# A mixture of experts in two stages: zero-filled half tile, early transposes, mask by expert, and first expert weights moved into the front stage

## Chip, cores and metric

One core of one Trainium2 chip runs the whole program. The metric is the device time of one execution in microseconds (us); less is better. The kernel of before took 2925.15 us, the median of three runs (2924.38 to 2936.98).

## What is computed

Input x has 16 sequences of 512 tokens with 256 features, 8192 tokens in all, in fp32. Four blocks follow each other:

```
x = x + attention(layernorm(x))        # 16 heads of 16
x = x + ffn(layernorm(x))
x = x + forget_attention(layernorm(x))
x = x + ffn(layernorm(x))              # the same weights again
```

The change concerns `ffn`, a mixture of E = 64 experts with F = 192 hidden features beside one shared expert with 192:

```
logits = x @ router_w.T;  the 8 largest of softmax(logits), normalised to sum 1
each expert takes the first 128 tokens (C = 128) that chose it, in order of tokens
y = (silu(xb @ w_gate) * (xb @ w_up)) @ w_down      # for each expert
out = sum over a token's experts of weight * y
    + (silu(x @ gate) * (x @ up)) @ ws_down         # shared expert
```

## The kernel before, in words

`program` calls seven stages one after the other; each has its own tiles, and all engines meet between two. `mixture` (L1755) is called twice and runs `moe_front` (tag m1f, later m2f) and `moe_experts` (m1e, m2e).

**`moe_front`** works in 16 rounds of 4 tiles of 128 tokens. Every engine walks the same steps s = 0 to 27 with the helper `in_turn`: for each step it goes through its own list of (step of item i, stage, number of items) and issues what is due. So the order of the list is the order of an engine's queue inside a step. Round i is loaded at step i, normalised and turned at i+1, has its logits at i+2 and its mask counted at i+3. The shared expert of round r runs gate and up at `shared_at(r)`, which is 2r+2 for the first eight rounds and r+10 for the others, and its down projection one step later. So in the first half (steps 2 to 18) even steps have gate and up and odd steps down; from step 19 on each step has one round of both, and two groups of four experts for the slot search.

The pieces: `turn_x` (L977) transposes x on TensorE in two halves of a round through the one bank `ps_x`; ScalarE's `keep` (L935) copies each half into `x_turned`, which holds all 8192 tokens. `logits` (L987) multiplies it by the router's weights. VectorE's `eight_largest`, `mark`, `shift` and `choose` (L866 to L883) make the 0/1 mask `chosen`, laid out as tile by expert. `count_tiles` (L996) sums the mask over tiles into `ps_c`, with `chosen` as the moving operand. `gate_up` (L1004) has 192 gate and 192 up features in three 128-wide groups; the third holds 64 of each. So `hidden` (L894) writes a product with 128 rows and one with 64, and `down` (L1016) contracts first over 128 rows (L1022), then over the 64 rows `hT[0:SR]` (L1023).

The slot search finds the token of each of 128 slots of each expert. `reach` (L902, VectorE) compares the counts with the slot numbers, 16 groups. `climb` (L1027, TensorE) multiplies an expert's mask, as weights, by two triangular tables, into `ps_x`; `copy_rise` (ScalarE) copies that; `find_place` (L1037) multiplies by `reached` into the one bank `ps_l`; `count_below` (L908, VectorE) reduces it. `count_reached` (L1046) multiplies `reached` by ones for all 64 experts, into `ps_c`, at step 20. The queue of SP carries the loads of x (`load`), the loads of the residual, the stores of the normalised rows with their gates, and the stores of the result. POOL sets constants first, then makes the inverse deviations, the gates and the last addition.

**`moe_experts`** handles 32 pairs of experts, pipelined by the lags of L1075: pair i's match of slots at step i+2, x turned at i+3, gate and up at i+4, h turned at i+5, down at i+6, scatter at i+7. SP loads a pair's weights (three DMAs of 384 KB, L1128 and L1129) into a ring of eight, as soon as down of eight pairs earlier is done. POOL gathers the 128 rows of each expert by an indirect DMA (L1139) and adds the outputs to the result in HBM by two indirect DMAs a pair (L1149). A scatter of pair i waits until all scatters before it have landed (L1146), and ScalarE's and VectorE's copies of y (a ring of four, YB) wait for the scatter of four pairs earlier. TensorE's order in a step is on L1202:

```
in_turn([(L_DOWN, down_second), (L_TURN, turn), (L_GU, gate_up(0)), (L_DOWN, down_first), (L_GU, gate_up(1)), (L_TURN_H, turn_h),
         (L_SAME, spread_first)])
```

`down_second` waits for ScalarE's copy of h (`copy_h`), which follows `turn_h` of the step before.

## Time and profile before

| What | us |
|---|---|
| median of 3 runs | 2925.15 |
| profiled execution | 2919.55 |
| its span | 2917.9 |
| TensorE matmuls busy | 2560.5 (88%) |
| VectorE busy | 1764.7 (60%) |
| ScalarE busy | 1255.0 (43%) |
| GpSimd busy | 1095.4 (38%) |

In the span, `moe_front` runs from 1247 to 1531 and from 2352 to 2629 us, `moe_experts` from 1534 to 1808 and from 2633 to the end. The other stages fill the rest. Engines in the rows: PE is TensorE's matmul, PEld its weight load, DVE is VectorE, ACT ScalarE, POOL GpSimd, and SPq SyncE's queue of DMA issues. A matmul in fp32 shows up as two records of each kind. A row's end of a matmul is modelled, so the distance from start to start says more than the duration. Some records of matmuls can be missing.

### The profile page before, as it was taken

To read this page: it belongs to the slowest core of one execution; us is meant where nothing else is said; L and a number is where in the kernel's file an instruction comes from. 1 tells how busy PE (TensorE), PEld (TensorE's weight loads), DVE (VectorE), ACT (ScalarE), POOL (GpSimd) and SP (SyncE) were. 2 spreads that over 40 slices of the span, in tenths; PEclk is the share of its full clock that TensorE was granted. 3 is DMA by queue.
4 is the path that set the end of the run, shared out by engine and by line. 5 is a ranking of instruction groups with operands and counts; after the bars stand their busy time and mean duration, and the time that the engine had idled before them with its cause. 6 is when DMAs were issued, how large, how long until landed. Compare 5 with 4: busy or idle time off the path is not lost. (4 is left out here: it accounts for less than half of the span.)

```text
span 2917.9 us, 46118 instructions
## 1 busy us (share of the span) xinstructions
PE 2560.5 (88%) x14506; PEld 1389.5 (48%) x14506; DVE 1764.7 (60%) x4173; ACT 1255.0 (43%) x2084; POOL 1095.4 (38%) x1246
## 2 busy tenths in 40 slices
PE   8996999999999899879997885799999979997885
PEld 5652233333333333345545653466666545555563
DVE  7995887877878778356522222588888657522221
ACT  3442565655666556523322221355555324322221
POOL 6885000000000000023224665477777623214665
PEclk9996899999999999979998997899999979998998
DMA  5556643554446534045329884011111035329884
GB/s 156 189 189 131 100 83 66 92 88 79 68 76 103 83 66 66 32 142 164 119 71 298 225 211 66 19 36 36 38 38 30 21 118 185 125 65 284 227 218 57
DMA packets 283225, 325.24 MB, mean 111 GB/s; under 512 B 22800, under 2 KB 264608, under 8 KB 283040
## 3 DMA queue, kind: packets, MB, share of 16 engines
q1 hardware_dynamic: 251392, 274.46, 37.8%
q0 software_dynamic: 27136, 46.16, 8.0%
q10 hardware_dynamic: 4512, 2.40, 0.3%
q8 instruction: 86, 1.41, 0.2%
q14 instruction: 99, 0.81, 0.1%
HBM read 217.23 MB, written 105.19 MB: 110 GB/s over the span
## 5 line engine op out<-in xcount | busy, mean ns | idle before, releaser
L591 DVE TENSOR_REDUCE a_row_max<-a_ps_m 128x1 f32<-128x512 f32 x1024 | 667.0, 688 | 194.6 <-PE a_ps_m L492 152.3
L646 ACT ACTIVATE a_probs<-a_ps_s 128x1024 f32<-128x1024 f32 x512 | 511.6, 1025 | 358.5 <-PE a_ps_s L516 269.3
L492 PE MATMUL a_ps_m<-a_ks,a_qs 96*128 96x512 bf16 x1024 | 411.2, 404 | 68.2 <-DVE a_row_max L591 40.0
L516 PE MATMUL a_ps_s<-a_qs,a_ks 98*128 98x512 bf16 x1024 | 315.0, 390 | 1.9 <-ACT a_probs L646 1.9
L492 PEld LDWEIGHTS a_ps_m<-a_ks,a_qs 96*128 96x128 bf16 x1024 | 99.9, 98 | 427.7 <-DVE a_row_max L591 380.4
L465 POOL COPY a_va<-a_vs 128x256 f32<-128x256 f32 x64 | 22.9, 402 | 735.2 <-DMA a_vs<-v 735.2
L534 PE MATMUL a_ps_o<-a_probs,a_va 128*32 128x512 f32 x2048 | 274.3, 608 | 2.1 <-ACT a_o_sb L655 1.7
L1419 POOL TENSOR_TENSOR b_spread<-b_decay,held_own_sb 128x512 f32<-128x512 f32 x256 | 269.2, 1086 | 8.7 <-DVE b_weight L1517 8.7
L1517 DVE TENSOR_TENSOR b_weight<-b_ps_s,b_spread 128x512 f32<-128x512 f32 x256 | 163.7, 682 | 17.9 <-PE b_ps_s L1652 17.9
L516 PEld LDWEIGHTS a_ps_s<-a_qs,a_ks 98*128 98x128 bf16 x1024 | 100.8, 100 | 75.8 <-ACT a_probs L646 12.7
L1254 DVE SCALAR_TENSOR_TENSOR m1e_h<-m1e_act_g,m1e_xg,m1e_ps_h 128x192 f32<-128x192 f32 x64 | 26.5, 415 | 164.7 <-ACT m1e_act_g L1216 164.7
L1254 DVE SCALAR_TENSOR_TENSOR m2e_h<-m2e_act_g,m2e_xg,m2e_ps_h 128x192 f32<-128x192 f32 x64 | 26.5, 414 | 164.7 <-ACT m2e_act_g L1216 164.7
L1642 PE MATMUL b_ps_p<-b_xnT,b_w_qk 128*128 128x512 f32 x256 | 121.3, 596 | 2.4 <-DVE b_q_bd L1503 2.2
L277 PE MATMUL a_ps_qk<-a_w_qk,a_xnT 128*128 128x512 f32 x256 | 122.2, 600 | 0.0
L1176 PE MATMUL m2e_ps_h<-m2e_w_gu,m2e_xgT 128*128 128x384 f32 x256 | 101.2, 522 | 0.0
L1176 PE MATMUL m1e_ps_h<-m1e_w_gu,m1e_xgT 128*128 128x384 f32 x256 | 100.6, 520 | 0.0
L1012 PE MATMUL m1f_ps_h<-m1f_x_turned,held_ws_gate_up_sb 128*128 128x512 f32 x192 | 96.1, 640 | 0.0
L471 POOL DMA_DIRECT2D x<-a_xo x32 | 23.5, 734 | 189.7 <-DVE a_xo L624 189.7
L1012 PE MATMUL m2f_ps_h<-m2f_x_turned,held_ws_gate_up_sb 128*128 128x512 f32 x192 | 94.1, 629 | 0.0
L1587 ACT ACTIVATE b_o_sb<-b_ps_o,b_den_eps 128x512 f32<-128x512 f32 x64 | 44.1, 689 | 110.9 <-PE b_ps_o L1662 110.9
L165 POOL TENSOR_TENSOR a_qk<-a_rot_cos,a_rot_sin 128x512 f32<-128x512 f32 x64 | 81.6, 1275 | 23.9 <-DVE a_rot_sin L208 23.9
L1149 POOL DMA_INDIRECT out_dram<-m2e_y,m2e_slots x32 | 51.6, 1613 | 81.4 <-DMA out_dram<-m2e_y,m_slots 51.0
(311 smaller groups left out, 5092.3 us busy)
## 6 DMA issues: line engine op xcount, KB each, us to landing
parts<-a_parts SPq DMA_DIRECT2D x16, 1536.0 KB, 6.2
a_qs<-parts SPq DMA_DIRECT2D x192, 128.0 KB, 7.4
a_ks<-parts SPq DMA_DIRECT2D x192, 128.0 KB, 10.0
m1e_w_gu<-in_L_ffn_w_gate_dram SPq DMA_DIRECT2D x32, 384.0 KB, 4.5
m1e_w_gu<-in_L_ffn_w_up_dram SPq DMA_DIRECT2D x32, 384.0 KB, 5.9
m1e_w_d<-in_L_ffn_w_down_dram SPq DMA_DIRECT2D x32, 384.0 KB, 7.7
m2e_w_gu<-in_L_ffn_w_gate_dram SPq DMA_DIRECT2D x32, 384.0 KB, 4.3
m2e_w_gu<-in_L_ffn_w_up_dram SPq DMA_DIRECT2D x32, 384.0 KB, 5.7
```

What stands on the lines that cost most here:

```text
L165: nc.gpsimd.tensor_tensor(qk[:, u, :], rot_cos[:, u, :], rot_sin[:, u, :], ALU.add).then_inc(qk_done, 1)
L277: last = nc.tensor.matmul(ps_qk[u][:], xnT[:, u, c, :], w_qk[:, c, :], start=c == 0, stop=c == 1)
L492: nc.tensor.matmul(ps_m[t % 2][:], qs[u][0:K_MAX, h, t * P:(t + 1) * P], ks[u][0:K_MAX, h, :], start=True, stop=True).then_inc(max_ready, 1)
L516: last = nc.tensor.matmul(ps_s[half][:, i, :], ks[u][0:K_ALL, h, t * P:(t + 1) * P], qs[u][0:K_ALL, h, :], start=True, stop=True)
L534: last = nc.tensor.matmul(ps_o[VW * j:VW * (j + 1), :], va[n.u][:, t, h * VW:(h + 1) * VW], probs[:, group % 2, j, t, :], start=t == 0, st ...
L591: nc.vector.tensor_reduce(row_max[:, n.u, t, n.h:n.h + 1], ps_m[t % 2][:], AX.X, ALU.max).then_inc(max_done, 1)
L646: nc.scalar.activation(probs[:, group % 2, n.h % 4, 2 * half:2 * half + 2, :], ps_s[half][:], ACT.Exp, scale=DK ** -0.5).then_inc(exp_done, 1)
L1012: last = nc.tensor.matmul(ps_h[i][:], w_gu[:, c, i, :], x_turned[:, c, r * S:(r + 1) * S], start=c == 0, stop=c == 1)
L1176: last = nc.tensor.matmul(ps_h[j][:], xgT[:, i % 2, j, c, :], w_gu[:, i % WB, j, :, c, :], start=c == 0, stop=c == C - 1)
L1419: nc.gpsimd.tensor_tensor(spread[:, n % 2, heads].rearrange("p h t c -> p (h t) c"), decay[:, n % 3, heads].rearrange("p h (t o) -> p (h t ...
L1517: nc.vector.tensor_tensor(weight[:, n % 2, heads, :], ps_s[r][:].rearrange("p h (j t) -> p (h j) t", t=P), spread[:, n % 2, heads].rearran ...
L1642: last = nc.tensor.matmul(ps_p[:], w_qk[:, c, blk * P:(blk + 1) * P], xnT[:, sg % 2, c, :], start=c == 0, stop=c == 1)
```

## The change

- In `moe_front` rows 64 to 127 of the second half of `hT` and of the shared down weights are set to zero on POOL, and the second down matmul contracts over 128 rows.
- `x_turned` becomes a ring of 10 rounds. This makes room for four pairs of expert weights, allotted outside both stages.
- `chosen` is laid out expert by tile. `climb` reads adjacent elements as weights, `count_tiles` strided ones as moving operand, and `choose` writes in the other order.
- `find_place` alternates between the banks `ps_l` and `ps_c` and waits for all of `reached`; `count_reached` moves to the last step and to `ps_x`.
- TensorE's order in a step of the front is another, with `turn_x` in front and `count_tiles` last.
- SP loads the weights of pairs 0 to 3 at steps 16, 18, 20 and 22 of the front.
- In `moe_experts` the ring has four pairs, loads begin with pair 4, and each also waits for x turned of the pair two before. TensorE's order begins with `spread_first` and `turn`.

```diff
-    XB, RB = 3, 4
+    XB, RB, HELD = 3, 4, 4
+    XT = 10
-        x_turned = sb("x_turned", [P, 2, T])
+        x_turned = sb("x_turned", [P, 2, XT * S])
-        chosen = sb("chosen", [P, 1 + TILES, E], bf16)
+        chosen = sb("chosen", [P, E, 1 + TILES], bf16)
-        ps_c = pb("ps_c", [P, 4, E])
+        ps_c = pb("ps_c", [P, TPR * P])
...
+            def load_weights(i):
+                for to, source in pair_of_weights(const, i, i):
+                    sp.dma_start(to, source).then_inc(w_loaded, 16)
+
-            in_turn([(lambda i: i, lambda i: load(i + XB - 1), ROUNDS - XB + 1), (shared_at, load_residual, ROUNDS),
+            in_turn([(lambda i: i, lambda i: load(i + XB - 1), ROUNDS - XB + 1), (lambda i: ROUNDS + 2 * i, load_weights, HELD),
+                     (shared_at, load_residual, ROUNDS),
                      (lambda i: i + L_GATE, store_rows, ROUNDS), (lambda r: shared_at(r) + 1, store, ROUNDS)])
             sp.wait_ge(pad_stored, 16)
+            sp.wait_ge(w_loaded, 48 * HELD)
...
             pool.wait_ge(setup, 7)
+            nc.gpsimd.memset(hT[SR:P, :, 1, :], 0.0).then_inc(setup, 1)
+            pool.wait_ge(setup, 8)
+            nc.gpsimd.memset(w_d[SR:P, 1, :], 0.0).then_inc(setup, 1)
+            pool.wait_ge(setup, 9)
...
-                nc.vector.tensor_scalar(chosen[:, 1 + TPR * s:1 + TPR * (s + 1), :], marked[:, s % 2], MARK / 2, None, ALU.is_lt).then_inc(chosen_done, 1)
+                nc.vector.tensor_scalar(chosen[:, :, 1 + TPR * s:1 + TPR * (s + 1)], marked[:, s % 2].rearrange("p t e -> p e t"), MARK / 2, None, ALU.is_lt).then_inc(chosen_done, 1)
...
                     act.wait_ge(x_was_turned, 2 * s + q + 1)
-                    first = (TPR * s + 2 * q) * P
+                    wait(act, gated, 3 * (s - XT + 1))
+                    first = (TPR * (s % XT) + 2 * q) * P
...
-                    last = nc.tensor.matmul(ps_c[0:E, 0, :], later_tiles[:, E - 1 - n:2 * E - 1 - n], chosen[:, 1 + n, :], start=n == 0, stop=n == TILES - 1)
+                    last = nc.tensor.matmul(ps_c[0:E, 0:E], later_tiles[:, E - 1 - n:2 * E - 1 - n], chosen[:, :, 1 + n], start=n == 0, stop=n == TILES - 1)
...
-                        last = nc.tensor.matmul(ps_d[q][:, t, :], hT[0:SR, r % 2, 1, at:at + P], w_d[0:SR, 1, :], start=False, stop=True)
+                        last = nc.tensor.matmul(ps_d[q][:, t, :], hT[:, r % 2, 1, at:at + P], w_d[:, 1, :], start=False, stop=True)
...
-                    nc.tensor.matmul(out, chosen[:, 1:1 + TILES, e], up_to[:], start=True, stop=False)
-                    last = nc.tensor.matmul(out, chosen[:, 0:TILES, e], past[:], start=False, stop=True)
+                    nc.tensor.matmul(out, chosen[:, e, 1:1 + TILES], up_to[:], start=True, stop=False)
+                    last = nc.tensor.matmul(out, chosen[:, e, 0:TILES], past[:], start=False, stop=True)
...
             def find_place(k):
                 pe.wait_ge(rise_done, k + 1)
-                pe.wait_ge(reached_done, k + 1)
-                wait(pe, below_done, GROUP * k)
+                pe.wait_ge(reached_done, GROUPS)
+                wait(pe, below_done, GROUP * (k - 1))
                 for j in range(GROUP):
                     e = GROUP * k + j
-                    last = nc.tensor.matmul(ps_l[:, j * P:(j + 1) * P], reached[:, e, :], rise[:, k % 2, j, :], start=True, stop=True)
+                    last = nc.tensor.matmul((ps_l, ps_c)[k % 2][:, j * P:(j + 1) * P], reached[:, e, :], rise[:, k % 2, j, :], start=True, stop=True)
                 last.then_inc(place_ready, 1)
 
             def count_reached(k):
-                pe.wait_ge(reached_done, GROUPS)
+                pe.wait_ge(rise_done, GROUPS)
                 for e in range(E):
-                    last = nc.tensor.matmul(ps_c[:, 1, e:e + 1], reached[:, e, :], ones[:], start=True, stop=True)
+                    last = nc.tensor.matmul(ps_x[:, 0, e:e + 1], reached[:, e, :], ones[:], start=True, stop=True)
...
-            in_turn([(lambda i: i + L_LOGITS, logits, ROUNDS), (even, climb, GROUPS), (down_at, down(0), ROUNDS), (lambda i: i + L_GATE, count_tiles, ROUNDS),
-                     (even, find_place, GROUPS), (odd, climb, GROUPS), (down_at, down(1), ROUNDS),
-                     (lambda i: i + L_NORM, turn_x(0), ROUNDS), (shared_at, gate_up(0), ROUNDS), (odd, find_place, GROUPS),
-                     (lambda i: i + L_NORM, turn_x(1), ROUNDS),
-                     (shared_at, gate_up(1), ROUNDS), (shared_at, gate_up(2), ROUNDS), (lambda i: COUNTED + 1, count_reached, 1)])
+            in_turn([(lambda i: i + L_LOGITS, logits, ROUNDS), (lambda i: i + L_NORM, turn_x(0), ROUNDS), (even, climb, GROUPS),
+                     (down_at, down(0), ROUNDS), (shared_at, gate_up(0), ROUNDS), (lambda i: i + L_NORM, turn_x(1), ROUNDS), (even, find_place, GROUPS),
+                     (odd, climb, GROUPS), (down_at, down(1), ROUNDS), (shared_at, gate_up(1), ROUNDS), (odd, find_place, GROUPS),
+                     (shared_at, gate_up(2), ROUNDS), (lambda i: i + L_GATE, count_tiles, ROUNDS), (lambda i: STEPS - 1, count_reached, 1)])
+def pair_of_weights(const, i, k):
+
+    two = slice(2 * i, 2 * i + 2)
+    for m, w in enumerate((const["w_gate"], const["w_up"])):
+        yield const["w_gu"][:, k, :, m], w[two].rearrange("e (p c) f -> p e c f", c=2)
+    yield const["w_d"][:, k], const["w_down"][two].rearrange("e (p c) d -> p e c d", c=2)
...
-    WB, XB, YB, DB = 8, 8, 4, 6
+    WB, XB, YB, DB = 4, 8, 4, 6
+    LEAD = 2
...
+            for i in range(WB, PAIRS):
                 k = i % WB
-                wait(sp, y0_ready, i - WB + 1)
...
+                sp.wait_ge(y0_ready, i - WB + 1)
+                sp.wait_ge(x_turned, i - LEAD + 1)
+                for to, source in pair_of_weights(const, i, k):
+                    sp.dma_start(to, source).then_inc(w_loaded[k], 16)
...
-            in_turn([(L_DOWN, down_second), (L_TURN, turn), (L_GU, gate_up(0)), (L_DOWN, down_first), (L_GU, gate_up(1)), (L_TURN_H, turn_h),
-                     (L_SAME, spread_first)])
+            in_turn([(L_SAME, spread_first), (L_TURN, turn), (L_DOWN, down_second), (L_GU, gate_up(0)), (L_DOWN, down_first), (L_GU, gate_up(1)),
+                     (L_TURN_H, turn_h)])
```

## Rows read from the trace of the kernel before

**Rows 1.** Busy us by stretches, second front: PE, PEld, DVE, ACT, POOL; clock, DMA share, GB/s.

```profile
2375.00:2400.00 25.00, 23.54 (x123) 14.68 (x122) 19.83 (x90) 8.44 (x13) 6.73 (x10) 1.00 0.50 158
2400.00:2425.00 25.00, 22.07 (x117) 14.72 (x117) 16.26 (x74) 11.76 (x19) 10.01 (x12) 0.93 0.50 164
...
2550.00:2575.00 25.00, 24.63 (x145) 13.97 (x142) 6.76 (x35) 6.40 (x12) 5.05 (x4) 1.00 0.19 62
```

**Rows 2.** Waits of TensorE, second front: total us, times, longest.

```profile
PE m2f_ps_x L983 <- DVE m2f_row L863: 7.2, 1, 7.2
PE m2f_ps_x L983 <- ACT m2f_x_turned L939: 6.2, 8, 0.8
PE m2f_ps_l L993 <- ACT m2f_x_turned L939: 5.5, 8, 0.7
...
PE m2f_ps_l L1043 <- DVE m2f_below L913: 2.6, 1, 2.6
```

**Rows 3.** Timeline of TensorE, first front, 1414 to 1424 us: start, us, what.

```profile
1413.94 5.42 PE L1012 MATMUL m1f_ps_h<-m1f_x_turned,held_ws_gate_up_sb 128*128 128x512 f32 x12
...
1419.56 0.27 PE L1033 MATMUL m1f_ps_x<-m1f_up_to,m1f_chosen 128*64 128x128 bf16 x1
1419.67 0.28 PE L1034 MATMUL m1f_ps_x<-m1f_past,m1f_chosen 128*64 128x128 bf16 x1
...
1421.39 0.70 PE L1023 MATMUL m1f_ps_d<-held_ws_down_sb,m1f_hT 64*128 64x256 f32 x2
1422.02 0.70 PE L1022 MATMUL m1f_ps_d<-held_ws_down_sb,m1f_hT 128*128 128x256 f32 x2
...
1423.18 0.38 PE L1043 MATMUL m1f_ps_l<-m1f_rise,m1f_reached 64*128 64x128 bf16 x4
```

**Rows 4.** Chain that ended last, in order of time, second expert stage.

```profile
2637.73 6.58 DMA m2e_xg<-rows,m_slots
...
2654.74 1.13 PE m2e_ps_y L1192 x4
...
2657.63 0.86 PE m2e_ps_y L1199 x4
2658.49 0.43 PE m2e_ps_y L1200 x2
...
2661.34 1.13 PE m2e_ps_y L1192 x4
```

**Rows 5.** Timeline of POOL, second expert stage: first scatters of pairs 0, 5, 22, 31.

```profile
2660.24 1.62 POOL L1149 DMA_INDIRECT out_dram<-m2e_y,m2e_slots  x1 [9.04 <-DVE m2e_y L1261]
...
2712.91 1.63 POOL L1149 DMA_INDIRECT out_dram<-m2e_y,m2e_slots  x1 [3.16 <-DMA out_dram<-m2e_y,m_slots]
...
2848.21 1.62 POOL L1149 DMA_INDIRECT out_dram<-m2e_y,m2e_slots  x1 [0.71 <-DVE m2e_slots L1246]
...
2906.45 1.56 POOL L1149 DMA_INDIRECT out_dram<-m2e_y,m2e_slots  x1 [3.07 <-DMA out_dram<-m2e_y,m_slots]
```

**Rows 6.** DMA queues, 2633 to 2918 us: packets, MB, share of 16 engines.

```profile
q1 hardware_dynamic: 24064, 37.75, 44.1%
q0 software_dynamic: 12288, 18.88, 35.3%
```

**Rows 7.** DMA issues, 2633 to 2700 us: KB each, median us to landing.

```profile
m2e_w_d<-in_L_ffn_w_down_dram SPq DMA_DIRECT2D x15, 384.0 KB, 14.8
```

**Rows 8.** DMA issues, 2850 to 2918 us: median us to landing.

```profile
out_dram<-m2e_y,m_slots POOLq DMA_INDIRECT x10, 3.8
...
m2e_xg<-rows,m_slots POOLq DMA_INDIRECT x6, 3.0
```

**Rows 9.** Timeline at the start of the second front, POOL.

```profile
2352.31 0.36 POOL L806 MEMSET m2f_zeros<- 128x320 f32 x1
```

**Rows 10.** Instructions on tile m2f_ps_x: ns min/median/max, first and last start, forms.

```profile
L983 PE MATMUL m2f_ps_x<-held_ident_sb,m2f_row x128: 272/273/475, 2360.6 to 2501.7; 128*128 128x128 f32 x128
```

**Rows 11.** Instructions of line 905, first front: ns min/median/max, first and last start.

```profile
L905 DVE TENSOR_TENSOR m1f_reached<-m1f_along,m1f_ps_c x16: 668/670/679, 1420.7 to 1429.7; 64x512 bf16<-64x512 f32 x16
```

More of the change, by code:

```diff
@@ L912, in count_below @@
                     wait(dve, below_done, e - 1)
-                    nc.vector.tensor_scalar(below[:, e % 2, :], ps_l[:, j * P:(j + 1) * P], spare_row[:], None, ALU.is_le, ALU.add,
+                    nc.vector.tensor_scalar(below[:, e % 2, :], (ps_l, ps_c)[k % 2][:, j * P:(j + 1) * P], spare_row[:], None, ALU.is_le, ALU.add,
                                             accum_out=count[:, e:e + 1]).then_inc(below_done, 1)
@@ L924, in _ @@
             dve.wait_ge(tiles_counted, 1)
-            nc.vector.scalar_tensor_tensor(number[:], ps_c[:, 1, :], float(P), count[:], ALU.mult, ALU.add).then_inc(number_done, 1)
+            nc.vector.scalar_tensor_tensor(number[:], ps_x[:, 0, 0:E], float(P), count[:], ALU.mult, ALU.add).then_inc(number_done, 1)
             dve.wait_ge(number_done, 1)
@@ L974, in _ @@
             pe.wait_ge(w_copied, 4)
-            pe.wait_ge(setup, 7)
+            pe.wait_ge(setup, 9)
             def turn_x(q):
@@ L990, in logits @@
                 for t in range(TPR):
[L991 removed]
+                    at = (TPR * (s % XT) + t) * P
                     for c in range(2):
@@ L1011, in stage @@
                     for c in range(2):
-                        last = nc.tensor.matmul(ps_h[i][:], w_gu[:, c, i, :], x_turned[:, c, r * S:(r + 1) * S], start=c == 0, stop=c == 1)
+                        last = nc.tensor.matmul(ps_h[i][:], w_gu[:, c, i, :], x_turned[:, c, r % XT * S:(r % XT + 1) * S], start=c == 0, stop=c == 1)
                     last.then_inc(gated, 1)
@@ L1123, in _ @@
         def _(sp):
-            def load(i):
+            for i in range(WB, PAIRS):
                 k = i % WB
-                wait(sp, y0_ready, i - WB + 1)
-                for m, w in enumerate((w_gate, w_up)):
-                    sp.dma_start(w_gu[:, k, :, m], w[2 * i:2 * i + 2].rearrange("e (p c) f -> p e c f", c=C)).then_inc(w_loaded[k], 16)
-                sp.dma_start(w_d[:, k], w_down[2 * i:2 * i + 2].rearrange("e (p c) d -> p e c d", c=C)).then_inc(w_loaded[k], 16)
-            in_turn([(0, load)])
+                sp.wait_ge(y0_ready, i - WB + 1)
+                sp.wait_ge(x_turned, i - LEAD + 1)
+                for to, source in pair_of_weights(const, i, k):
+                    sp.dma_start(to, source).then_inc(w_loaded[k], 16)
         @block.gpsimd
@@ L1171, in stage @@
                     if j == 0:
-                        pe.wait_ge(w_loaded[i % WB], 48 * (i // WB + 1))
+                        wait(pe, w_loaded[i % WB], 48 * (i // WB))
                         pe.wait_ge(xT_done, i + 1)
```

20 lines of the change are left out of this document (10 added, 10 removed).

## The prediction

> **What bounds the kernel now.** The profiled execution took 2919.55 us, span 2917.9, 5.6 us under the median of the runs (2925.15); I work against it and add 5.6 at the end. The change touches two functions, each used twice: the front of the mixture and its expert stage. I take the second use of each. First the busy time by stretches [rows 1]: in the front TensorE is busy for 22 to 24.6 of every 25 us, VectorE for up to 19.8. A busy row need not be a full engine, so the waits and timelines decide.
>
> The front, 2352 to 2629 us, is TensorE's queue. Of its idle time the change touches [rows 2] 6.2 and 5.5 us for ScalarE's copy of the turned x and 2.6 for `count_below`. The matmuls hide more. Gate and up take 5.42 us for twelve records of 512 columns, 0.45 each; a record of 256 should need 0.22. The down projection takes 0.63 us for a matmul (two records), 0.31 a record [rows 3]; here a 128-row matmul follows a 64-row one every time. In the expert stage two matmuls with the same 256 columns over 96 rows take 0.86 and the one over 128 rows behind them 0.43, that is 0.215 a record [rows 4]. So each change between 64 and 128 rows costs 0.63 - 0.43 = 0.20 us.
>
> The expert stage is a serial chain on POOL's queue: two scatters of pair i, two gathers, and scatter i+1 waits until scatter i has landed. The first scatters of pairs 0, 5, 22 and 31 start at 2660.24, 2712.91, 2848.21 and 2906.45 [rows 5]: 10.5 us a pair, then 7.96, then 6.47. The landing sets this: weights move through the first two stretches (q1 has the most engine time [rows 6], a weight load takes 14.8 us to land [rows 7]); in the last stretch they have all come, and a scatter lands in 3.8 [rows 8]. 1.93 from one issue to the next, 3.8 and some 0.75 to restart make 6.5. TensorE, where it runs free, needs 2661.34 - 2654.74 = 6.6 us a pair [rows 4].
>
> **The change, part by part.** *64 rows made 128.* 16 rounds x 8 matmuls = 128 changes of row count a front, 64 in each half: -12.8 us a half. The price is two POOL memsets: 0.36 us for 320 columns [rows 9] gives 1.15 for 1024 and 0.3 for 256. They end by 2355, and POOL is first needed once x has come and its statistics are made: TensorE waits 7.2 us for the first normalised rows [rows 2], so nothing is paid.
>
> *x turned early (first half, steps 2 to 18).* A turn no longer follows the other turn, nor logits the second turn: down, gate or count lie between. That takes away 6.2 + 5.5 = 11.7 us. But `normalise` must be done 2 us earlier. Now a pair of rounds takes 18.8 us (32 half rounds turned from 2360.6 to 2501.7 [rows 10]), and VectorE is busy for 36.1 of 50 [rows 1], 13.6 us a pair. TensorE's pair becomes 18.8 - 1.6 - 1.5 + 0.4 = 16.1: VectorE has 2.5 us to spare, some of which goes to its own waits for SiLU and rstd. I take 2 us a front for this coupling, bounds 0 and 10.
>
> *Mask by expert.* `climb` now loads adjacent weights. Its records start 0.11 us apart for 64 columns lying 128 bytes apart; `find_place`, with adjacent ones, goes at (0.38 - 0.216)/3 = 0.055 [rows 3]. The even climbs stand right before down(0), which waits for `hidden` of the step before and now waits longer by what they save; 7 odd climbs x 8 x 0.055 = -3.1 us. In return `count_tiles` streams 64 elements 130 bytes apart. No row shows such a moving operand; nearest are `climb`'s weights. Bounds 0 and +0.055 for each of 64; I take the upper, +3.5 us, as the read is of the same kind. `choose` on VectorE also gets a strided output: up to its own time again, 16 x 0.3, inside the coupling's bound. The Trainium skill, "SBUF — State Buffer", on cachelines, says that a read which goes to another 16-byte line at each element pays for it: a rule that helps `climb` and hurts `count_tiles`. Rows 3 agree for weights; for a moving operand no row here does, and if only weights paid, the two fronts would end 7 us lower.
>
> *Places in two banks, all heads reached first.* `find_place(0)` now waits for all 16 `reach`, which run from 1420.7 to 1430.4 [rows 11]. TensorE has only climb, down(0) and gate(0) before it, to about 1423.4, and waits 7 us; before it waited 2.6 at `find_place(1)`. Behind it in the queue are matmuls whose buffers are free. Both orders leave VectorE's 9.7 us in charge: step 19 saves nothing, +0.7 since `counted` comes later.
>
> *Second half:* 7 steps x 1.6 = -11.2, climbs -3.1, `count_reached` moved to the tail -1.6 + 0.6, step 19 +0.7: -14.6. *First half:* -12.8 - 11.7 + 3.5 + 2 = -19.0. A front: **-33.6**, two: -67. Bounds -25 (coupling 10) and -44 (strided read free, and a granted clock of 1.00 where a window has 0.93).
>
> *Ring of 10 rounds.* The copy of round s waits for gate and up of s-10: round 15, step 16, needs round 5, done at step 12. No cost.
>
> *First weights in the front.* 12 DMA issues on SP at steps 16 to 22, where the DMA share is 0.19 [rows 1]. Behind them stand the residual load, needed a step (over 10 us) later, and the stores. 4.7 MB in 50 us: free, and SP's added wait at the end is met by then.
>
> *Experts.* Before, eight pairs of weights are asked for at once, and an early gather takes 6.58 us to land [rows 4] against 3.0 when none move [rows 8]: -4 us before the first scatter. Then 28 loads follow, one a pair. Before, scatters 0 to 22 carried loads; now 0 to about 25. Bounded by engine time (q1 44.1% and q0 35.3% of 285 us [rows 6]: 3.93 us a load; 3.14 a pair, by bytes 1.75 for gathers and 1.39 for scatters): 28 x 3.93 + 24 x 1.75 + 25 x 1.39 = 187, at nine tenths 207, then 6 x 6.47: scatter 31 at 2656 + 246 = 2902, -4. Bounded by the chain, 25 x 7.96 + 39 = 238: 2894, -12. I take -8 a stage, two: **-16**; bounds 0 and -15. TensorE's new order hides its wait for the copy of h, but TensorE isn't what ends last. The ring of four asks for pair i after down of pair i-4 and needs it 1.75 steps later, 11 to 14 us; where a load takes 14.8 [rows 7], the loop of two steps (13) plus landing gives 28 for four pairs, 7.0 each, still under the chain's 7.96: hidden. The second condition, x turned of pair i-2, is met earlier.
>
> Sum: 2919.55 - 67 - 16 = 2836.5; with 5.6, **2842 us**.
>
> **Rivals.**
> *Zero-filling brings nothing.* If the down matmuls keep 0.63 us at 128 rows, 4 x 12.8 = 51 us are missing: 2893. Rows 4, with 0.43 at 96 and 128 rows, speak against it. Chance 0.04. The Trainium skill, "TensorE: Matmul & The Clock Gate", Part 3, says that a weight load overlaps a running matmul only where the row group differs, which alone would bring this about; rows 4 contradict it.
> *VectorE becomes the bound of the first half.* 13.6 busy, its waits and a slower `choose` make a pair 17.1 instead of 16.1: +1 x 8 x 2, 2858. Chance 0.13.
> *The expert stage gives nothing.* The bytes are the same, and loads that went early now lie beside scatters 23 to 25: 2858. Chance 0.11.
> *More:* strided read free, steadier clock, experts at the chain's rate: -7 - 12 - 8, 2815. Chance 0.13.
> *Slower: four pairs of weights are too few.* Place: the wait at `gate_up(0)`. It decides once landing exceeds 4 x 7.96 - 13 = 19 us, and the whole change loses where it costs over 83 us in 56 pairs: 9.5 us a pair, landing above 25. The busiest stretch has 14.8. 2940, chance 0.02.
>
> **How the numbers follow.** Forecast 0.57. From 2842 the range takes in a coupled VectorE together with a stage that gives little (2872) and the better case with its bounds (2808). About 0.5%, 15 us, is what a measurement of this kernel can tell from no change: faster 0.95, same 0.03 (zero-fill and experts both fail), slower 0.02.
>
> **What would show it.** Down matmuls all over 128 rows, 0.43 apart; no wait of TensorE for the turned x; `climb` at 0.055, `count_tiles` near 0.1; one wait of 6 to 7 us at `find_place(0)`; each front some 33 us shorter; the first scatter 22 us after the first gather, the 10.5 us a pair gone, 6.5 only for the last six. A wait of TensorE for weights, or TensorE waiting for `normalise` round after round, would make it wrong.

## The result and the profile after

| | before | after |
|---|---|---|
| median of 4 runs | 2924.77 us (2922.16 to 2936.98) | 2845.89 us (2839.47 to 2847.92) |
| ratio | | 0.9734 [0.9697, 0.977] |
| profiled execution, span | 2919.55, 2917.9 us | 2839.47, 2837.8 us |
| mean granted clock of TensorE | 0.934 | 0.942 |

Faster by 2.7%; the forecast was 2842 us, range 2808 to 2872. The total is right to 4 us. What matters is whether its terms are.

So the span is cut at events that both traces have. A front has a lead (start of the stage to the first turn of x), a first half (H1, to the first climb) and a second half (H2, to the last number of the slots). An expert stage runs from its first gather to the first scatter of its last pair, and is cut at the first scatters of pairs 0, 5, 22 and 31, as in [rows 5]. In us:

| | front 1: H1, H2, all | front 2: H1, H2, all | experts 1: fill, 0-5, 5-22, 22-31, all | experts 2 | rest |
|---|---|---|---|---|---|
| before | 163.1, 110.8, 282.6 | 157.2, 110.9, 276.5 | 26.8, 51.2, 133.1, 58.2, 269.4 | 26.4, 52.7, 135.3, 58.2, 272.6 | 1816.8 |
| after | 144.8, 99.4, 252.6 | 141.9, 99.7, 250.0 | 26.5, 36.8, 133.1, 65.8, 262.3 | 25.8, 36.5, 135.2, 64.1, 261.6 | 1811.3 |
| gain | 18.3, 11.4, 30.0 | 15.3, 11.2, 26.5 | 0.3, 14.4, 0, -7.6, 7.1 | 0.6, 16.2, 0.1, -5.9, 11.0 | 5.5 |

The gains add up to 80.1 us. The fronts gave 56 where 67 was forecast, the experts 18 where 16 was, and 5.5 came from stages that the change doesn't touch.

Part of this is TensorE's granted clock. In these traces it has two levels, 2.4 GHz (1.0, the full one) and 1.2 GHz (0.5). In the second front of the changed kernel the gate and up matmuls of 512 columns start 0.43 us apart at the full level and 0.85 at the lower one, so a stretch at the lower level costs half its length where TensorE sets the time. It does so in H1: in six of the kernels below TensorE, VectorE and POOL do the same work in the front, and their twelve H1 take 141.0 to 147.9 us, with 11.3 to 25.4 us at the lower level. Less half of that, all twelve are 135.2 to 135.4. A time from which half its stretch at the lower level is taken off is called "at full clock" from here on.

| us, front 1 and front 2 | H1 | of it at 1.2 GHz | H1 at full clock | H2 | of it at 1.2 GHz | H2 at full clock |
|---|---|---|---|---|---|---|
| before | 163.1, 157.2 | 31.8, 19.6 | 147.2, 147.4 | 110.8, 110.9 | 3.4, 3.4 | 109.1, 109.2 |
| after | 144.8, 141.9 | 19.1, 13.3 | 135.3, 135.3 | 99.4, 99.7 | 6.8, 6.8 | 96.0, 96.3 |

So at full clock H1 is shorter by 12.0 us and H2 by 13.0. The other 6.4 and 3.2 us of the gains in H1 are the clock's, and H2 lost 1.7 to it. In the stages that the change doesn't touch TensorE was at the lower level for 200.0 us before and 185.9 after; half the difference is 7.0, near their 5.5.

Against [rows 3], the timeline of TensorE in the second front, H2:

```profile
2459.63 0.62 PE L1013 MATMUL m2f_ps_c<-m2f_chosen,m2f_later_tiles 128*64 128x64 bf16 x4
2460.07 0.24 PE L1046 MATMUL m2f_ps_x<-m2f_up_to,m2f_chosen 128*64 128x128 bf16 x1
2460.14 0.22 PE L1047 MATMUL m2f_ps_x<-m2f_past,m2f_chosen 128*64 128x128 bf16 x1
2460.20 0.22 PE L1046 MATMUL m2f_ps_x<-m2f_up_to,m2f_chosen 128*64 128x128 bf16 x1
...
2461.64 0.60 PE L1036 MATMUL m2f_ps_d<-held_ws_down_sb,m2f_hT 128*128 128x256 f32 x2
2462.07 0.59 PE L1035 MATMUL m2f_ps_d<-held_ws_down_sb,m2f_hT 128*128 128x256 f32 x2
2462.50 0.60 PE L1036 MATMUL m2f_ps_d<-held_ws_down_sb,m2f_hT 128*128 128x256 f32 x2
2462.93 1.45 PE L1025 MATMUL m2f_ps_h<-m2f_x_turned,held_ws_gate_up_sb 128*128 128x512 f32 x3
```

All down matmuls cover 128 rows and start 0.43 us apart instead of 0.63. The climbs go at 0.06 instead of 0.11, and `count_tiles`, whose moving operand is now strided, takes 0.44 for four, 0.11 each. All three were forecast.

Against [rows 2], the waits of TensorE in the second front (total us, times, longest):

```profile
PE m2f_ps_x L996 <- DVE m2f_row L875: 12.3, 9, 7.2
PE m2f_ps_d L1035 <- DVE m2f_hT L912: 6.3, 8, 0.8
PE m2f_ps_l L1056 <- DVE m2f_reached L917: 6.1, 1, 6.1
...
PE m2f_ps_x L996 <- ACT m2f_x_turned L952: 0.8, 1, 0.8
PE m2f_ps_l L1006 <- ACT m2f_x_turned L952: 0.7, 1, 0.7
```

The waits for the turned x have shrunk from 6.2 and 5.5 to 0.8 and 0.7. The one wait at `find_place(0)`, for all that is reached, is 6.1. The first row is the news: TensorE waits nine times for the normalised rows, where before it waited once, for the first ones. The 5.1 us of the other eight are what the prediction named as a sign against it. They lie in H1, so against [rows 1], busy us in 100 us of H1 of the second front (PE, PEld, DVE, ACT, POOL; clock, DMA share, GB/s):

```profile
2338.00:2438.00 100.00, 95.90 (x510) 68.18 (x509) 93.33 (x369) 48.51 (x74) 37.92 (x48) 0.98 0.60 198
```

The same stretch of the kernel before:

```profile
2375.00:2475.00 100.00, 92.67 (x459) 57.94 (x458) 73.50 (x330) 39.81 (x61) 31.86 (x42) 0.97 0.55 176
```

VectorE went from 73.5 to 93.3 us of 100. The pace rose by a ninth (459 to 510 records of TensorE), which takes VectorE to about 82; the other 11 us are new. The groups of its instructions in the window of after (busy us, mean ns, idle time before it) name them:

```profile
L875 DVE TENSOR_SCALAR m2f_row<-m2f_x,m2f_mean_var,m2f_rstd 128x256 f32<-128x256 f32 x48 | 29.6, 676 | 3.1 <-POOL m2f_rstd L831 3.1
...
L895 DVE TENSOR_SCALAR m2f_chosen<-m2f_marked 128x256 bf16<-128x256 f32 x12 | 4.7, 393 | 0.4
```

The same group in the window of before:

```profile
L863 DVE TENSOR_SCALAR m2f_row<-m2f_x,m2f_mean_var,m2f_rstd 128x256 f32<-128x256 f32 x44 | 16.5, 435 | 2.6 <-POOL m2f_rstd L819 2.6
```

`normalise` is the same instruction with the same operands, and its mean went from 435 to 676 ns. The timeline of VectorE in the kernel after shows where:

```profile
2366.49 1.37 DVE L875 TENSOR_SCALAR m2f_row<-m2f_x,m2f_mean_var,m2f_rstd 128x256 f32<-128x256 f32 x4
2373.14 3.57 DVE L875 TENSOR_SCALAR m2f_row<-m2f_x,m2f_mean_var,m2f_rstd 128x256 f32<-128x256 f32 x4 [0.52 <-POOL m2f_rstd L831]
2382.69 1.37 DVE L875 TENSOR_SCALAR m2f_row<-m2f_x,m2f_mean_var,m2f_rstd 128x256 f32<-128x256 f32 x4
```

The timeline of POOL beside it, its additions:

```profile
2357.45 2.59 POOL L844 TENSOR_TENSOR m2f_xo<-m2f_xo,m2f_xr 128x512 f32<-128x512 f32 x2
2373.65 2.59 POOL L844 TENSOR_TENSOR m2f_xo<-m2f_xo,m2f_xr 128x512 f32<-128x512 f32 x2
```

Every second time the four instructions take 3.57 us instead of 1.37, and POOL's addition of the residual runs right then. That is a coincidence in time, not yet a cause; two experiments below test it. Of the four, the second and the third are the long ones, 1.35 and 1.36 us, and each ends 0.15 us after one of the two additions. The first takes 0.70 and ends 0.15 after `gates` on POOL (0.61 us long). So it is all through the two fronts: the 42 executions of `normalise` over 0.6 us end 0.15 or 0.16 us after a POOL instruction.

A pair of rounds takes 2373.65 - 2357.45 = 16.2 us.

Against [rows 5], first scatters of pairs 0, 5, 22 and 31 in the second expert stage:

```profile
2590.53 1.62 POOL L1167 DMA_INDIRECT out_dram<-m2e_y,m2e_slots  x1 [8.42 <-DVE m2e_y L1279]
...
2627.03 1.63 POOL L1167 DMA_INDIRECT out_dram<-m2e_y,m2e_slots  x1 [1.55 <-DVE m2e_slots L1264]
...
2762.28 1.62 POOL L1167 DMA_INDIRECT out_dram<-m2e_y,m2e_slots  x1 [0.32 <-issue]
...
2826.35 1.56 POOL L1167 DMA_INDIRECT out_dram<-m2e_y,m2e_slots  x1 [2.90 <-DMA out_dram<-m2e_y,m_slots]
```

The 10.5 us a pair are 7.3; the middle is as it was; the last nine pairs cost 7.1 each instead of 6.5.

### The profile page after: what moved, and what is told of

The parts are those of the page before. It is cut to its first block and busy times, and to the rows that moved or that the text cites. A ratio compares the mean times of both kernels' runs of the same rounds, so it can differ in the third digit from the quotient of the medians.

```text
span 2837.8 us, 46202 instructions
## 1 busy us (share of the span) xinstructions
PE 2492.0 (88%) x14506; PEld 1385.6 (49%) x14506; DVE 1792.7 (63%) x4173; ACT 1246.7 (44%) x2084; POOL 1097.9 (39%) x1250
## 5 line engine op out<-in xcount | busy, mean ns | idle before, releaser
L492 PE MATMUL a_ps_m<-a_ks,a_qs 96*128 96x512 bf16 x1024 | 409.7, 402 | 68.9 <-DVE a_row_max L591 40.3
L1437 POOL TENSOR_TENSOR b_spread<-b_decay,held_own_sb 128x512 f32<-128x512 f32 x256 | 269.0, 1084 | 8.7 <-DVE b_weight L1535 8.7
L1535 DVE TENSOR_TENSOR b_weight<-b_ps_s,b_spread 128x512 f32<-128x512 f32 x256 | 163.8, 682 | 17.9 <-PE b_ps_s L1670 17.9
L1272 DVE SCALAR_TENSOR_TENSOR m1e_h<-m1e_act_g,m1e_xg,m1e_ps_h 128x192 f32<-128x192 f32 x64 | 26.5, 414 | 163.7 <-ACT m1e_act_g L1234 131.1
L1272 DVE SCALAR_TENSOR_TENSOR m2e_h<-m2e_act_g,m2e_xg,m2e_ps_h 128x192 f32<-128x192 f32 x64 | 26.5, 414 | 163.5 <-ACT m2e_act_g L1234 134.5
L1194 PE MATMUL m1e_ps_h<-m_w_gu,m1e_xgT 128*128 128x384 f32 x256 | 98.5, 511 | 0.0
L1194 PE MATMUL m2e_ps_h<-m_w_gu,m2e_xgT 128*128 128x384 f32 x256 | 97.3, 506 | 0.0
L534 PEld LDWEIGHTS a_ps_o<-a_probs,a_va 128*32 128x32 f32 x2048 | 40.6, 108 | 83.9 <-issue 83.6
```

What stands on the lines that cost most here:

```text
L492: nc.tensor.matmul(ps_m[t % 2][:], qs[u][0:K_MAX, h, t * P:(t + 1) * P], ks[u][0:K_MAX, h, :], start=True, stop=True).then_inc(max_ready, 1)
L534: last = nc.tensor.matmul(ps_o[VW * j:VW * (j + 1), :], va[n.u][:, t, h * VW:(h + 1) * VW], probs[:, group % 2, j, t, :], start=t == 0, st ...
L1194: last = nc.tensor.matmul(ps_h[j][:], xgT[:, i % 2, j, c, :], w_gu[:, i % WB, j, :, c, :], start=c == 0, stop=c == C - 1)
L1437: nc.gpsimd.tensor_tensor(spread[:, n % 2, heads].rearrange("p h t c -> p (h t) c"), decay[:, n % 3, heads].rearrange("p h (t o) -> p (h t ...
L1535: nc.vector.tensor_tensor(weight[:, n % 2, heads, :], ps_s[r][:].rearrange("p h (j t) -> p (h j) t", t=P), spread[:, n % 2, heads].rearran ...
```

## The experiments

Each kernel is the changed one with the edit shown. The theory: zero rows, early turns and the strided reads act as priced; VectorE, slowed by POOL's addition, holds TensorE up in H1; and in the expert stage the loads in the front pay and held-back ones cost at the end. The rivals are named in the expectations.

### Which part of the front brings what

**64 rows again.**

```diff
-  matmul(ps_d[q][:, t, :], hT[:, r % 2, 1, at:at + P], w_d[:, 1, :], ...)
+  matmul(ps_d[q][:, t, :], hT[0:SR, r % 2, 1, at:at + P], w_d[0:SR, 1, :], ...)
```

> The changed kernel with the second down matmul back at 64 rows. Mine: each change of row count costs 0.20 us, 64 in a second half, all on the path: +12.8 us. In the first half VectorE sets the pace at 16.2 us a pair of rounds, TensorE needs 15.5, so 1.6 more there shows as 0.9: +7. A front +20, both +40: about 2886 us, down matmuls 0.63 us apart. If TensorE sets the pace everywhere: +51, 2897. If weight loads stay uncovered at 128 rows anyway: 2846, no change.

2864.57 us, 0.981 [0.9759, 0.9862]. H2 is 114.1 and 114.4, longer by 14.7 each; H1 is 144.3 and 145.0, hardly moved. The timeline of its TensorE has the old distance back, 0.63 from start to start:

```profile
2517.49 0.70 PE L1036 MATMUL m2f_ps_d<-held_ws_down_sb,m2f_hT 64*128 64x256 f32 x2
2518.11 0.70 PE L1035 MATMUL m2f_ps_d<-held_ws_down_sb,m2f_hT 128*128 128x256 f32 x2
2518.74 0.70 PE L1036 MATMUL m2f_ps_d<-held_ws_down_sb,m2f_hT 64*128 64x256 f32 x2
```

So the zero-filling works. Of the 14.7, 11.3 are left at full clock (107.3 and 107.6 against 96.0 and 96.3); the rest is the clock, at the lower level for 13.7 us of this H2 and for 6.8 of the other. In H1 the times at full clock are 139.7 in both fronts against 135.3: 4.4 us of the 12.8 priced are seen. A pair of rounds takes 16.6 us here, in which TensorE is never idle, and 16.2 in the changed kernel, of which TensorE waits 0.65 for normalised rows: most of what the zeros save, it spends waiting. The measured H1 hides even the 4.4, since this kernel has only 9.2 and 10.6 us at the lower level there.

**The zero-filling alone** (all other parts taken back, so this is the kernel before with the zeros and 128 rows; the edit shows three of the places).

```diff
-  in_turn([... logits, turn_x(0), climb, down(0), gate_up(0), turn_x(1), find_place, climb, down(1), ...])
+  in_turn([... logits, climb, down(0), count_tiles, find_place, climb, down(1), turn_x(0), gate_up(0), ...])
...
-  chosen = sb("chosen", [P, E, 1 + TILES], bf16)
+  chosen = sb("chosen", [P, 1 + TILES, E], bf16)
...
-  WB, XB, YB, DB = 4, 8, 4, 6
+  WB, XB, YB, DB = 8, 8, 4, 6
```

> The kernel before with nothing but the zero fill and 128 rows in the down matmul. Mine: there TensorE's pair of rounds is 18.8 us and VectorE has slack, so all 256 changes count: 2925 - 51 = 2874 us. If VectorE sets the pace of the first half also here (its 16.2 us a pair): the same, since 17.2 is above it. If 128 rows bring nothing: 2925.

2894.05 us, 0.9896 [0.9848, 0.9944]. Against before, H1 is shorter by 8.4 and 2.0, H2 by 7.3 and 7.1, where 12.8 was priced for each. The clock hides a part: H1 has 36.3 and 37.5 us at the lower level, H2 6.8. At full clock H1 is shorter by 10.7 and 10.9, H2 by 9.0 and 8.9. The size is off too. In the even stretch of H2 a step, from one first down matmul to the next, takes 12.36 us (2548.19 to 2560.55) against 13.61 before (2565.74 to 2579.35), so 1.25 is saved, 6 changes of 0.20 and not 8. In the old order `find_place`, whose stationary operand has 64 rows, stands right behind the first four down matmuls, the last of which had 64 rows too. There was no change between them, and with zeros there is one: a step goes from 10 changes to 4, not to 2. In the new order the down matmuls have neighbours of 128 rows on both sides, so from the kernel with 64 rows to the changed one all 8 go, and such a step falls from 13.46 to 11.89, by 1.57; seven such steps make 11.0 of the 11.3 above. In this form too `normalise` meets POOL's addition and takes 653 ns in the mean, but here TensorE doesn't wait for it: its waits in H1 are those of before.

**x turned late again** (the old order of TensorE's queue in the front, all else kept).

> The changed kernel with TensorE's order in a front step as before (turns late, count_tiles early). Mine: the waits for the turned x come back, 11.7 us a front, but VectorE is relieved, since its normalise no longer meets POOL's addition (0.40 us each again instead of 0.64 in the mean): TensorE's pair 15.5 + 1.5 = 17.0 against 16.2 now, +6 a front, +13 in all, 2859. If VectorE plays no part: +23, 2869.

2864.73 us, 0.9801 [0.9756, 0.9846]. H1 158.8 and 157.6, H2 102.9 and 101.9: by time the new order is worth 15 us in H1 and 3 in H2. But this H1 has 36.1 and 32.9 us at the lower level; at full clock it is 140.8 and 141.1, and the order is worth 5.5 and 5.9 against the changed kernel (and 11.6 and 11.9 against the kernel below whose addition comes after `normalise`). The waits for the turned x are back to the tenth:

```profile
PE m2f_ps_x L996 <- ACT m2f_x_turned L952: 6.2, 8, 0.8
PE m2f_ps_l L1006 <- ACT m2f_x_turned L952: 5.5, 8, 0.7
```

**The mask by tile again.**

```diff
-  chosen = sb("chosen", [P, E, 1 + TILES], bf16)
+  chosen = sb("chosen", [P, 1 + TILES, E], bf16)
```

> The changed kernel with the mask laid out tile by expert again. count_tiles goes from 0.11 to 0.04 us each, climb from 0.055 to 0.11. Mine: in the first half VectorE sets the pace, so count_tiles' 4.5 us are not won; in the second half the odd climbs lose 3.1 a front: +6, 2852. If TensorE sets the pace in the first half: 2 x (-4.5 + 3.1) = -3, 2843.

2849.89 us, 0.9743 [0.9687, 0.9799]: not to be told from the changed kernel by its time, but by stages it is. H2 is 103.2 and 103.7, longer by 4 (3.1 were priced). H1 is 145.4 and 143.2, at full clock 133.6 in both: of the 3.5 us by which `count_tiles` should have been cheaper 1.7 appear, and TensorE's idle time in H1 grows from 6.6 to 9.3 us.

### What holds H1: the addition beside `normalise`

**The addition after `normalise`.** POOL adds the residual of round r, one of the first eight, a step later and only when VectorE is through with the normalised rows of that step. The edit shows the wait; its place in POOL's queue moves too.

```diff
 def add(r):
+    if r < EARLY:
+        pool.wait_ge(xn_done, TPR * min(shared_at(r) + 2, ROUNDS))
     pool.wait_ge(xr_loaded[r % 2], 16 * (r // 2 + 1))
```

> The changed kernel with POOL's additions of the first eight rounds put one step later, and only after that step's normalise. Mine: the slow normalises (3.6 us for four instead of 1.4, once a pair of rounds) come from POOL adding at the same time; they go, all 64 are near 0.40 us, VectorE's pair falls from 16.2 to 14 us and TensorE's 15.5 sets the pace: the first half 5 us shorter in each front, -11, 2835. If the slow ones have another cause: they stay slow, 2846 or more.

2825.37 us, 0.9692 [0.9659, 0.9726]. H1 falls to 135.1 and 134.1, by 9.7 and 7.8, more than expected. At full clock it is 129.2 in both fronts, 6.1 less than in the changed kernel; the rest is the clock, which doesn't fall after the first 20 us of this H1 and had 10.2 and 3.4 us at the lower level there in the changed one. A pair of rounds takes 15.3 us, `normalise` 442 ns, and in the stretch below TensorE has no idle time left. Busy us in 100 us of H1, this kernel:

```profile
2327.00:2427.00 100.00, 100.00 (x550) 71.71 (x548) 92.53 (x391) 52.47 (x80) 41.95 (x53) 1.00 0.63 206
```

Its groups of VectorE there:

```profile
L878 DVE TENSOR_SCALAR m2f_row<-m2f_x,m2f_mean_var,m2f_rstd 128x256 f32<-128x256 f32 x52 | 19.9, 442 | 3.6 <-POOL m2f_rstd L831 3.6
...
L898 DVE TENSOR_SCALAR m2f_chosen<-m2f_marked 128x256 bf16<-128x256 f32 x14 | 10.7, 761 | 0.5
```

On VectorE the cost was halved, not removed, but TensorE no longer waits for it. The addition now meets `choose`, the other VectorE instruction of this kind with one source in SBUF, and its mean doubles from 393 to 761 ns. The timeline of VectorE at one such place:

```profile
2348.44 0.41 DVE L893 TENSOR_TENSOR m2f_logit<-m2f_ps_l,m2f_top 128x256 f32<-128x256 f32 x1
2348.88 1.13 DVE L898 TENSOR_SCALAR m2f_chosen<-m2f_marked 128x256 bf16<-128x256 f32 x1
2349.93 1.39 DVE L864 BATCH_NORM_STATS2 m2f_stats<-m2f_x 128x6 f32<-128x256 f32 x4
```

And POOL's addition at that place:

```profile
2347.28 2.49 POOL L846 TENSOR_TENSOR m2f_xo<-m2f_xo,m2f_xr 128x512 f32<-128x512 f32 x2 [1.20 <-DVE m2f_row L878]
```

The subtraction that has its logits in PSUM starts while the addition runs and takes its usual 0.41; `choose` right behind it takes 1.13 and ends 0.24 us after the addition. The Trainium skill, "SBUF — State Buffer", section "Who interferes with whom", says that a `tensor_scalar` from SBUF to SBUF can use a port pair which VectorE shares with GpSimd, and that whoever comes second is then blocked for the whole instruction. The trace agrees: the four `normalise` take 2.2 us longer beside two additions of 1.3, and one alone has up to 1.36 us where it takes 0.40 undisturbed. What is left above 403, the median of `normalise` (its mean is 435 before and 442 here), are those beside `gates`, 7 of 64 in a front: 0.70 us, ending 0.15 us after it, before and here.

**No addition at all in the front.** One of 256 features is added, so that the residual is left out of the output for the others; all waits stay.

```diff
-  nc.gpsimd.tensor_tensor(half, half, xr[:, r % 2, 2 * q:2 * q + 2, :], ALU.add)
+  nc.gpsimd.tensor_tensor(half[:, :, 0:1], half[:, :, 0:1], xr[:, r % 2, 2 * q:2 * q + 2, 0:1], ALU.add)
```

> The changed kernel where POOL adds only one of the 256 features of the residual, so that its addition takes next to no time; the rest of the residual is left out of the output. Mine: every normalise near 0.40 us, first half as in the kernel with the additions moved (5 us shorter a front) or a little better: 2833. If POOL's additions don't slow VectorE: no normalise changes, 2846.

2827.82 us, 0.9711 [0.9665, 0.9757]; H1 133.7 and 134.3, `normalise` 445 ns. The addition is the cause: without its work, and with its semaphores in place, H1 is within 1.4 us of the kernel that only moves it, and at full clock 129.3 against 129.2.

VectorE doesn't set the pace of the changed kernel by itself. Single pairs of its second front, one at full clock and one with a stretch at the lower, and one of the kernel with the addition after `normalise`:

```profile
2391.40:2407.60 16.20, 15.55 (x85) 11.08 (x85) 15.34 (x61) 7.95 (x12) 6.33 (x9) 1.00 0.64 212
2423.80:2441.60 17.80, 17.14 (x85) 11.90 (x85) 15.42 (x61) 7.95 (x12) 6.31 (x9) 0.91 0.40 133
```

```profile
2364.30:2379.60 15.30, 15.30 (x86) 10.95 (x85) 14.15 (x61) 7.95 (x12) 6.24 (x9) 1.00 0.69 224
```

VectorE has the same 15.4 us of work in the first two, but the pair is 1.6 longer where TensorE runs slower, and TensorE still waits its 0.66 for the rows. So the two wait for each other in turn: TensorE's own 15.3 us a pair are on the path, and the slow `normalise` adds 0.9.

H1 at full clock, from one kernel to the next: 147.3 before, 136.5 with the zeros alone, 141.0 with all but the new order, 129.2 with the order and the addition out of the way, 135.3 as changed. The clock itself goes with the waits, though not strictly. Where TensorE never waits after the start of H1 (64 rows, addition moved or gone) the clock doesn't fall again after the first 20 us. Where TensorE waits 0.65 us once a pair the clock falls up to four times, for 3.4 us each; where it waits 1.5 us a pair (before, the zeros alone, the late turns) the clock is at the lower level for 10 to 27 us.

### What holds the expert stage

**Nothing fetched in the front**: the ring keeps four pairs, and all loads start with the stage.

```diff
-  (shared_at, load_residual, ROUNDS), (lambda i: ROUNDS + 2 * i, load_weights, HELD)
+  (shared_at, load_residual, ROUNDS)
...
-  for i in range(WB, PAIRS):
+  for i in range(PAIRS):
```

> The changed kernel with the first four pairs' weights fetched at the start of the expert stage again, ring of four and all else as changed. Mine: what the stage won (11 us in each) is DMA time moved out of it; 4 loads of 3.93 us come back beside the first gathers and scatters: +8 a stage, +16, 2862. If the loads are hidden behind the gathers and TensorE's slow start: 2846.

2850.81 us, 0.9758 [0.9695, 0.9821]; stages 266.6 and 265.8, fill 28.4 and 27.5, pairs 0-5 41.4 and 35.7. The slow start of the old stage doesn't come back, although every weight is fetched in the stage. Nor does the old order of TensorE bring it back (below). What is left is eight pairs asked for at once; four asked for at once do no such harm. This is by exclusion, as no run asks for eight in the changed kernel; the transfers agree: from 2660 to 2713 us before, the queue of the weights moved 12.08 MB beside scatters 0 to 5, in the changed kernel (2590 to 2627) 6.32. The loads in the front themselves seem worth 4 us a stage, but that is not shown: six kernels here share the changed kernel's expert stage (it, 64 rows, late turns, mask by tile, the two with the addition moved or gone), and their twelve stages take 258.1 to 267.0.

**A ring of eight, the first four pairs from the front**; the other loads aren't held back.

```diff
-  WB, XB, YB, DB = 4, 8, 4, 6
+  WB, XB, YB, DB = 8, 8, 4, 6
...
-  sp.wait_ge(y0_ready, i - WB + 1)
-  sp.wait_ge(x_turned, i - LEAD + 1)
+  wait(sp, y0_ready, i - WB + 1)
```

> The changed kernel with a ring of eight pairs: 0 to 3 from the front, 4 to 7 asked for at the start of the expert stage, the rest eight ahead. Mine: the same 28 loads in the stage, only earlier: the first scatters are slower (above 8 us a pair), the last ones free of loads: within 3 us of 2846. If holding the loads back is what won: +8 a stage, 2862.

2830.86 us, 0.9696 [0.9631, 0.9761]; stages 256.2 and 255.5, the best of all. Its first scatters of pairs 0, 5, 22 and 31:

```profile
2586.31 1.62 POOL L1171 DMA_INDIRECT out_dram<-m2e_y,m2e_slots  x1 [10.50 <-DVE m2e_y L1283]
...
2622.81 1.63 POOL L1171 DMA_INDIRECT out_dram<-m2e_y,m2e_slots  x1 [1.44 <-DVE m2e_slots L1268]
...
2754.94 1.62 POOL L1171 DMA_INDIRECT out_dram<-m2e_y,m2e_slots  x1 [1.20 <-issue]
...
2813.96 1.56 POOL L1171 DMA_INDIRECT out_dram<-m2e_y,m2e_slots  x1 [3.06 <-DMA out_dram<-m2e_y,m_slots]
```

Pairs 0 to 5 take 36.5 as in the changed kernel, and the last nine 59.0 instead of 64.1: with eight pairs held, the last load is asked for four pairs earlier, and the tail runs free of it. The ring of four costs 6 us at the end and doesn't help the start.

**The same ring with a wait between the loads**, each after x of pair i-4 is turned.

```diff
+  sp.wait_ge(x_turned, i - HELD + 1)
```

> The changed kernel with a ring of eight pairs whose loads for pairs 4 to 7 go out one at a time, each after x of four pairs earlier is turned. The plain ring of eight filled in 28 us against 26 and ended 6.5 us earlier (scatters 22 to 31 in 58.6 against 65). Mine: both, fill 25 and end 58.6: stage 8 us shorter than in the changed kernel, -16, 2830. If the fill depends on other things: -12, 2834. If the early loads only move the slowness forward (scatters 0 to 5 above 45 us): 2840.

2835.46 us, 0.9722 [0.9689, 0.9755]; pairs 0-5 40.1 and 40.3, stages 264.0 and 256.8. Spacing brings nothing; in the first stage it may even cost. The last nine pairs take 59.4 and 59.2, as without it, so it is the depth of the ring that frees the tail, not that loads aren't held back.

**The old order of TensorE in the expert stage**, and **only `spread_first` at its old place**.

```diff
-  [spread_first, turn, down_second, gate_up(0), down_first, gate_up(1), turn_h]
+  [down_second, turn, gate_up(0), down_first, gate_up(1), turn_h, spread_first]
...
+  [turn, down_second, gate_up(0), down_first, gate_up(1), turn_h, spread_first]
```

> The changed kernel with TensorE's order in an expert step as before. Its new wait for VectorE's match of slots (20 us a stage) goes, the wait for the copy of h (15 us) returns. Mine: TensorE isn't the bound but for the filling of the pipeline, where the new wait cost some 3 us before the first scatter: -3 a stage, 2840. If TensorE's waits don't reach the scatters: 2846.

> The changed kernel with TensorE's order turn, down_second, gate_up(0), down_first, gate_up(1), turn_h, spread_first: neither wait should remain for more than 0.3 us a pair. Mine: pace in the filled pipeline 6.2 to 6.4 us a pair where TensorE runs free, first scatter 3 us earlier; the rest is the scatters' chain: -3 to -5 a stage, 2838. If nothing reaches the scatters: 2846.

2855.41 us, 0.977 [0.9707, 0.9833], stages 270.3 and 269.9; and 2854.33 us, 0.9775 [0.9711, 0.9838], stages 269.0 and 263.7. With the old order TensorE waits 17.3 us for the copy of h, as before (15.4), and both stages are longer than any of the twelve, by 3 us at least and 8 against the changed kernel: the new order seems worth that, so TensorE isn't wholly off the path. These two stages also have 55 us each at the lower clock, against 40 in the changed kernel; which makes which wasn't separated. With only `spread_first` back at its place the wait for `match` is gone, and the stage is no shorter. The three times lie within 0.5% of each other, so by time alone none of this is separated.

### Both edits that helped

**The addition after `normalise` and the spaced ring of eight** (the diffs of those two).

> Both: spaced ring of eight and additions after normalise. They touch different stages, so they add: 2846 - 16 - 11 = 2819. If either fails, 2830 to 2835.

2815.34 us (2809.8 to 2821.06), 0.9663 [0.9629, 0.9696]: 30 us less than the changed kernel by time, and some 20 by the ratios, since the kernel before took 2916.19 us beside these runs and 2924.77 beside the changed one. (In the same way the addition after `normalise` gives 20 us by time and 12 by ratio.) H1 is 134.8 and 134.0, and all four times lie below those of either edit alone. Its expert stages, 259.8 and 264.3, are those of the spaced ring; without the spacing it was not run.

## Why the prediction was right, and where it was not

**The total: right, in part by luck.** For the fronts 67 us were forecast. At full clock they gave 50, and the clock, which the forecast left as it was but for one bound, 6 more; the stages that weren't touched gave 5.5 and the experts 2 above their 16.

**Zero rows: the mechanism right, the term mis-sized.** "7 steps x 1.6", and 12.8 in H1, count the eight changes that 64 rows cause between neighbours of 128. Before, one neighbour was `find_place` with 64 rows, so the change leaves 4 of 10 where the prediction took 8 away: 6 x 0.20 = 1.2. A step fell from 13.61 to 11.89, by 1.7, of which 0.5 is the climb; 1.6 and 0.44 were priced. H2 was to give 14.6 and gave 11.4 and 11.2, at full clock 13.0: 9 for the zeros alone and 4 for the mask. So of the 3.3 us missing 1.7 are the clock's and 1.6 the terms'. In H1, where the sum had 12.8, the zeros alone give 10.8 at full clock. The rival that zero rows bring nothing is refuted by the 0.43 between matmuls of 128 rows with different weights. The rule of the Trainium skill ("TensorE: Matmul & The Clock Gate", Part 3), that a weight load overlaps only where row groups differ, doesn't hold here: each of these matmuls has its own weight load over the same 128 rows, and two records of 256 columns at 0.22 fill the 0.43.

**Turns early: right.** The waits of 11.7 us went to 1.5. At full clock the order is worth 11.6 and 11.9 in H1 where TensorE doesn't wait for `normalise`, and 5.5 and 5.9 in the changed kernel, where it does. The 15 by time hold 9 us of clock.

**Mask by expert: right.** Climbs at 0.055 and a strided moving operand at 0.11 each for 64 columns, the upper bound that was taken; H2 gained 4. In H1 1.7 of the 3.5 priced are seen against the kernel with the mask by tile. From the zeros alone to the late turns, which have the new layout (and the new banks and rings), H1 grows by 4.5 at full clock, so the price was rather low.

**H1: near the right sum by luck.** 19.0 was forecast and 18.3 and 15.3 came, but 12.0 at full clock; 6.4 and 3.2 were the clock's. The steps said that TensorE would set the pace with 16.1 us a pair of rounds. It is 16.2, but not for that reason. The 18.8 that the sum started from held stretches at the lower clock; a pair of before without one takes 17.9, so the same sum gives 15.2, and TensorE alone does take 15.3. The failing step is "VectorE has 2.5 us to spare", 13.6 busy in a pair: it took VectorE's durations as fixed. The coupling, put at 2 us a front with bounds 0 and 10, costs 6.1 at full clock, and 8 to 10 with the clock that goes with it. Before, the addition waits for ScalarE's copy of the down product, and starts 0.6 us after `normalise` has ended; after, the copy is there first. The two rows of the timelines of before, VectorE and POOL, with this gap (2400.87 + 1.66 = 2402.53):

```profile
2400.87 1.66 DVE L863 TENSOR_SCALAR m2f_row<-m2f_x,m2f_mean_var,m2f_rstd 128x256 f32<-128x256 f32 x4 [0.52 <-POOL m2f_rstd L819]
...
2403.15 2.49 POOL L832 TENSOR_TENSOR m2f_xo<-m2f_xo,m2f_xr 128x512 f32<-128x512 f32 x2 [1.74 <-ACT m2f_xo L958]
```

No row of before had the two together, and the shorter steps brought them there. The rival that VectorE becomes the bound was near in its mechanism, as VectorE and TensorE came to wait for each other, and wrong in its cause and price: it put the pair at 17.1.

**Places in two banks: right.** One wait of 6.1 (7 was forecast); the wait of 2.6 at `find_place(1)` is gone. The waits of `down` for `hidden` went from 2.6 to 6.3, which the prediction has too.

**Memsets, ring of ten rounds, loads on SP: nothing, as said.** The lead is 8.4 us after and 8.6 before.

**Experts: the sum near (18 for 16), the steps half.** The 10.5 us a pair went, as forecast. "First scatter 22 us after the first gather" failed: it stayed at 26. The first turn of x comes 4.3 us after the first gather instead of 7.9, but the first scatter then comes 21.5 us later instead of 18.5. The waits of TensorE in the second expert stage show the new one:

```profile
PE m2e_ps_r L1177 <- DVE m2e_same L1259: 19.6, 26, 2.1
PE m2e_ps_x L1184 <- DMA m2e_xg<-rows,m_slots: 11.1, 5, 4.1
...
PE m2e_ps_y L1210 <- ACT m2e_hT L1240: 2.3, 4, 0.7
```

`spread_first` now stands first in the step and waits for `match`, 2.1 us of it in the fill, while the wait for the copy of h fell from 15.4 to 2.3. The first gates of the stage take 5.11 us against 2.75 for the next pair, at the lower of the two clocks, as they did before (5.06). How much of the fill each has is open: in the twelve stages that are alike it varies from 23.0 to 29.5, and the shortest has 9.7 us at the lower clock in it, the longest 16.6. At the other end loads now lie beside the scatters until the last six pairs, which was priced; what wasn't seen is that a ring of eight avoids it. As the prediction has it, the runs leave only the burst of eight pairs as what made the start slow; the one without loads in the front shows that they aren't needed to cure it. The bounds 0 and -15 beside the term of -16 can only be meant for one stage, where 7.1 and 11.0 came.

**Four pairs of weights too few: refuted.** TensorE waits for no weight load in either stage.
